# Clearing the record grid, loading the inputs and counting the cells differently in a graph kernel on one Trainium2 core

## The chip, the cores and the metric

The kernel runs on one core of one Trainium2 chip. The metric is the device time of one execution in microseconds (us); of several runs the median is taken. The engines are called as in the profile: PE (matrix multiply), DVE (vector), ACT (scalar), POOL (GpSimd) and SP (the sync engine, which here only issues DMAs). PE's clock has two levels, 1.2 and 2.4 GHz; the profile gives the granted clock of a stretch as a share of the higher one.

## The reference

A graph of 6250 nodes and 200,000 edges, 48 features a node. Cut to what matters:

```
h = relu(layernorm(x))
# first network: a gated message pass, then 4 attention layers over the edges src <- dst
gate = silu(edge_attr @ F1W + F1b) @ F2W + F2b + embedding term of (src, dst)
h = ln(h + segment_sum(gate * h[dst] * cutoff * mult[dst], src) / total)
for i in range(4):
    score = (Q[src] * K[dst]).sum() + 0.1 * (edge_attr * Q[src][:, :40]).sum() + log(mult[dst])
    alpha = segment_softmax(score, src)
    h = ln(h + leaky(concat(h, segment_sum(alpha * h[dst] @ Wm[i], src)) @ Wu[i]))
x = x + h
# second network: 5 steps of a degree-normalised spread over the same edges
out = x + spread(relu(layernorm(x)))
```

## The kernel before, in words

The nodes are cut into 49 blocks of 128 (NB = 49). Each edge belongs to a cell, given by the block of its source and the block of its target, so there are 49 x 49 cells. In device memory stands a grid of records (REC) with room for 128 edges in each cell; a record (RW = 54 floats) holds the edge's 40 attributes and its fields. Everything after the preparation (gate pass, attention layers, spread) reads this grid. The preparation is what the change touches, and it runs through these stages, in the order of the calls at the end of the program:

- load_all (L407 to L465): DVE clears six tiles (L414 to L419), then SP loads 22 pieces of input and weights (L420 to L440). Then come two iotas on POOL, small constants on DVE (L441 to L454), and a few matrix products and reductions on the weights (L456 to L463).
- count_cells (L468 to L545): a tile of zeros is set (L470, 128 x 2646 floats), the edges' sources, targets and weights are loaded (L471 to L473, each 125 partitions x 1600 elements), and DVE takes local index and block number out of them (L474 to L490). Then the histogram: for 200 groups of 8 edge columns, DVE makes two one-hot tiles by comparing a row 0..48 with the block numbers (L503, L504), and PE multiplies them, one product per column (L512, 1600 in all). Two buffers for each tile let DVE run ahead of PE. From the histogram DVE works out base positions (L519 to L539). Then SP writes the zeros tile to the grid, one block row after the other (L541, L542: 49 DMAs of 1323 KB), and one small piece (L543).
- fill_extra (L552): two barriers over all five engines, with a loop between them that runs only where cells overflow.
- place_edges (L561 to L659): 200 iterations. In each, PE and DVE work out the slots of 8 x 125 edges (L594 to L649), ACT copies attributes and fields together into rec_out (L590, L591, from attr_in, which SP loads in 20 pieces, L578), and POOL scatters 8 x 125 records into the grid with 8 indirect DMAs (L655). A slot tile may be at most four iterations ahead of the scatters (L647, L648). A barrier ends it.

What sets the order: nearly all of load_all and count_cells goes through a helper, serial. It numbers the steps by a single semaphore, order, and each step waits until every step before it, on whatever engine, has ended:

```
for who, fn, inc in steps:
    if who == name:
        e.wait_ge(order, count[0])
        fn(e).then_inc(order, inc)
    count[0] += inc
```

A DMA counts 16, and ends when its data have landed. So every DMA of these stages is issued only after the one before it has landed, and the following compute waits for them all. The histogram and place_edges use semaphores of their own.

Of the kernel before, what the change touches and what calls it, by code (L numbers as in the profile page):

```python
# [11 lines left out]
P = 128  # L12
NB = -(-N // P)
# [5 lines left out]
NS = 8  # L19
SC = ET // NS  # L20
# [20 lines left out]
def build(nc, x, src, dst, edge_attr_40, edge_weight, node_type_119, node_vec, Wq, gq, bq, Wk, gk, bk, Wm, Wu, go,  # L41
# [11 lines left out]
    with ctx:  # L53
        def sem(name):
            return ctx.enter_context(nc.semaphore(name))
# [6 lines left out]
        s_hpe, s_hdve = sem("hist_pe"), sem("hist_dve")  # L62
        s_aload = [sem(f"adj_loaded_{k}") for k in range(2)]
# [135 lines left out]
        with scope() as st:  # L199
# [9 lines left out]
            one_bs, one_bd = sb(st, "one_bs", [EP, 2, NS, NB], BF16), sb(st, "one_bd", [EP, 2, NS, NB], BF16)  # L209
# [13 lines left out]
            zeros = sb(st, "zeros", [P, NB * RW])  # L223
# [114 lines left out]
        def program(name, e):  # L338
# [68 lines left out]
            def load_all():  # L407
# [4 lines left out]
                wqk = WQK[:, :, :].rearrange("i l (k o) -> i (l k) o", k=2)  # L412
                steps = [
                    v(lambda e: e.memset(X[:, :, :], 0.0)),  # L414
# [5 lines left out]
                    sy(lambda e: e.dma_start(X[:, 0:NB - 1, :], x_main)),  # L420
                    sy(lambda e: e.dma_start(X[0:TAIL, NB - 1, :], x[(NB - 1) * P:N, :])),
                    sy(lambda e: e.dma_start(MULT[0:TAIL, NB - 1:NB], node_vec[(NB - 1) * P:N].rearrange("(p o) -> p o", o=1))),
                ]
                def mult_main(e):
                    with nc.allow_non_contiguous_dma(reason="one column of node values per block"):
                        return e.dma_start(MULT[:, 0:NB - 1], node_vec[0:(NB - 1) * P].rearrange("(b p) -> p b", p=P))
                steps.append(sy(mult_main))
                for n, w in enumerate((gq, gk, bq, bk, go, bo)):
                    steps.append(sy(lambda e, n=n, w=w: e.dma_start(LP[:, n, :, :].rearrange("p l h -> p (l h)"), flat(w))))
                steps += [  # L430
                    sy(lambda e: e.dma_start(GN[:, 0, :], vec(gn))), sy(lambda e: e.dma_start(GN[:, 1, :], vec(bn))),
                    sy(lambda e: e.dma_start(WQK[:, :, 0:H], Wq.rearrange("l i o -> i l o"))),
                    sy(lambda e: e.dma_start(WQK[:, :, H:2 * H], Wk.rearrange("l i o -> i l o"))),
                    sy(lambda e: e.dma_start(WM[:, :, :], Wm.rearrange("l i o -> i l o"))),
                    sy(lambda e: e.dma_start(WUF[0:H, :, :], Wu[:, 0:H, :].rearrange("l i o -> i l o"))),
                    sy(lambda e: e.dma_start(WU2[:, :, :], Wu[:, H:2 * H, :].rearrange("l i o -> i l o"))),
                    sy(lambda e: e.dma_start(F1[0:RBF, 0:H], F1W)), sy(lambda e: e.dma_start(F2[0:H, :], F2W)),
                    sy(lambda e: e.dma_start(F2[H:KW, :], F2b.rearrange("(o h) -> o h", o=1))),
                    sy(lambda e: e.dma_start(F1B[:, :], col(F1b))),
                    sy(lambda e: e.dma_start(F2B[:, :], F2b.rearrange("(o h) -> o h", o=1))),  # L440
# [13 lines left out]
                    v(lambda e: e.memset(DEG[:, :], 1.0)),  # L454

                    t(many([lambda e, l=l: e.transpose(bank(0)[0:H, l * H:(l + 1) * H], WM[:, l, :], ident[0:H, 0:H]) for l in range(L)])),  # L456
# [7 lines left out]
                ]  # L464
                serial(steps)  # L465


            def count_cells():  # L468
                serial([
                    v(lambda e: e.memset(zeros[:, :], 0.0)),  # L470
                    sy(lambda e: e.dma_start(src_i[:, :], src.rearrange("(p t) -> p t", t=ET))),  # L471
                    sy(lambda e: e.dma_start(dst_i[:, :], dst.rearrange("(p t) -> p t", t=ET))),
                    sy(lambda e: e.dma_start(home[:, :], edge_weight.rearrange("(p t) -> p t", t=ET))),  # L473
                    v(lambda e: e.tensor_copy(fields[:, :, 2], home[:, :])),  # L474
                ])
                for raw, local, block_f, fb in ((src_i, 0, bs_f, 3), (dst_i, 1, bd_f, 4)):
# [16 lines left out]
                HG = NS  # L493
                groups = ET // HG
                iota49 = lambda n: iota_f[0:EP, 0:NB].unsqueeze(1).broadcast_to([EP, n, NB])
                if name == "vector":
                    e.tensor_scalar(iota_f[:, :], iota_f[:, :], 1.0, None, ALU.subtract).then_inc(s_hdve, 1)
                    e.wait_ge(s_hdve, 1)
                    for g in range(groups):
                        if g >= 2:  # L500
                            e.wait_ge(s_hpe, g - 1)
                        c0 = g * HG
                        e.tensor_tensor(one_bs[:, g % 2], iota49(HG), bs_f[:, c0:c0 + HG].unsqueeze(2).broadcast_to([EP, HG, NB]), ALU.is_equal)  # L503
                        e.tensor_tensor(one_bd[:, g % 2], iota49(HG), bd_f[:, c0:c0 + HG].unsqueeze(2).broadcast_to([EP, HG, NB]), ALU.is_equal).then_inc(s_hdve, 1)  # L504
                    e.wait_ge(s_hpe, groups)
                if name == "tensor":
                    for g in range(groups):
                        e.wait_ge(s_hdve, g + 2)
# [52 lines left out]
            def place_edges():  # L561
# [88 lines left out]
                if name == "gpsimd":  # L650
                    for i in range(ITER):
# [1283 lines left out]
            count_cells()  # L1935
            fill_extra()
# [43 lines left out]
```

## Time and profile before

| | us |
|---|---|
| median of 3 runs | 11522.38 (11522.14 to 11533.53) |
| the profiled execution, its own time | 11514.63 |
| its span in the trace | 11512.8 |
| POOL busy | 5678.4 (49%) |
| DVE busy | 7579.4 (66%) |
| PE busy | 9029.0 (78%) |

The span is the time between the first and the last instruction of the profiled execution. Busy times are sums over instructions; an engine that waits is not busy. In the views below a time at the front of a line is the start, counted from the beginning of the span.

### The profile page before, as it was taken

What the parts mean: (1) busy time and instruction counts of PE and PEld (TensorE: products, weight loads), DVE (VectorE), ACT (ScalarE), POOL (GpSimd) and SP (SyncE); (2) the same over time, 40 slices, a digit from 0 to 9 for tenths busy, and PEclk for the clock granted to TensorE, in tenths of its full rate; (3) what the DMA queues carried; (4) which work ended last, traced back from release to release, by engine and by line L of the source; (5) the groups of instructions that cost most, each with busy time, mean ns of one, the idle gap of its engine ahead of it and who ended that gap; (6) DMA issues with size and microseconds to landing.
All of it is one profiled execution on the core that took longest, in us unless ns stands there. A gap on an engine that the chain in (4) does not pass through costs nothing. (4 is left out here: it accounts for less than half of the span.)

```text
span 11512.8 us, 361357 instructions
## 1 busy us (share of the span) xinstructions
PE 9029.0 (78%) x152213; PEld 8186.6 (71%) x152213; DVE 7579.4 (66%) x17807; ACT 4774.7 (41%) x14433; POOL 5678.4 (49%) x7141
## 2 busy tenths in 40 slices
PE   3166666666388888888888599979978997998899
PEld 2165555555377777777777499869978996998899
DVE  6176666666477777777777677667767776776211
ACT  0000000000144444444444377757766775777000
POOL 0077777777222222222222277757756774776000
PEclk9955555555699999999999799979979997998899
DMA  0511111111122222222222267647736773775565
GB/s 16 240 34 31 36 31 32 35 31 31 37 72 76 71 70 74 74 71 70 73 75 71 69 218 220 195 135 218 224 111 217 219 220 106 220 224 166 221 251 221
DMA packets 874542, 1382.84 MB, mean 120 GB/s; under 512 B 120770, under 2 KB 753314, under 8 KB 855769
## 3 DMA queue, kind: packets, MB, share of 16 engines
q1 hardware_dynamic: 796112, 1314.50, 34.1%
q0 software_dynamic: 76800, 45.06, 2.7%
q8 instruction: 1211, 19.84, 0.7%
q14 instruction: 419, 3.43, 0.1%
HBM read 1079.46 MB, written 278.06 MB: 118 GB/s over the span
## 5 line engine op out<-in xcount | busy, mean ns | idle before, releaser
L655 POOL DMA_INDIRECT edge_records<-rec_out,slot_i x1600 | 1910.6, 1194 | 991.8 <-issue 991.5
L1696 ACT ACTIVATE vals<-carry_h,weight 128x49 f32<-128x49 f32 x9604 | 2321.1, 327 | 6.4
L1533 PE MATMUL psum<-TT,hd_t 128*128 128x97 bf16 x28812 | 1538.3, 210 | 148.0 <-DMA hs_t<-one_hots 110.0
L1331 POOL TENSOR_TENSOR vals_g<-vals_g 128x343 f32<-128x343 f32 x343 | 527.3, 1537 | 2216.4 <-ACT vals_g L1314 2216.4
L1533 PEld LDWEIGHTS psum<-TT,hd_t 128*128 128x128 fp8e4 x28812 | 1374.8, 99 | 165.6 <-issue 162.7
L1741 POOL TENSOR_TENSOR vals<-vals 128x343 f32<-128x343 f32 x1372 | 1042.0, 759 | 92.9
L1294 ACT ACTIVATE hots<-psum 128x896 fp8e4<-128x896 f32 x686 | 629.0, 917 | 1040.3 <-PE psum L1138 651.2
L1736 POOL TENSOR_TENSOR vals<-vals 128x343 f32<-128x343 f32 x1372 | 1042.3, 760 | 6.8 <-ACT vals L1696 6.8
L1601 DVE SCALAR_TENSOR_TENSOR xks<-recs,psum 128x343 f32<-128x343 f32 x1372 | 697.0, 508 | 496.7 <-PE psum L1536 486.6
L1536 PE MATMUL psum<-ts,hs_t 128*128 128x49 bf16 x28812 | 985.3, 185 | 44.0 <-issue 43.6
L590 ACT COPY rec_out<-attr_in 125x320 f32<-125x320 f32 x200 | 91.0, 455 | 2185.4 <-DMA edge_records<-rec_out,slot_i 2185.4
L1573 PE MATMUL psum<-vals,hs 128*128 128x147 bf16 x9604 | 885.3, 235 | 45.4 <-POOL vals L1741 23.0
L1261 DVE TENSOR_TENSOR same<-psum,before_e 128x896 fp8e4<-128x896 f32 x343 | 374.5, 1092 | 826.1 <-PE psum L1163 826.1
L1536 PEld LDWEIGHTS psum<-ts,hs_t 128*128 128x128 fp8e4 x28812 | 879.7, 96 | 51.0 <-issue 50.6
L601 PE MATMUL psum<-ident,key_f 125*125 125x125 f32 x1600 | 690.9, 432 | 235.0 <-POOLq L354 235.0
L1682 ACT COPY carry_h<-psum 128x336 f32<-128x336 f32 x1372 | 590.9, 431 | 611.8 <-DVE xks L1601 608.4
L1899 PE MATMUL psum<-g,AJ 128*128 128x144 bf16 x12005 | 762.3, 228 | 73.1 <-POOLq L354 73.1
L1899 PEld LDWEIGHTS psum<-g,AJ 128*128 128x128 fp8e4 x12005 | 761.4, 99 | 74.0 <-POOLq L354 74.0
L607 PE MATMUL psum<-one_bd,one_bs 125*49 125x49 bf16 x1600 | 106.4, 218 | 831.4 <-DVE one_bsT L622 831.4
L610 PE MATMUL psum<-base,one_bsT 49*125 49x98 f32 x3200 | 727.9, 418 | 0.0
L607 PEld LDWEIGHTS psum<-one_bd,one_bs 125*49 125x49 bf16 x1600 | 81.9, 132 | 908.2 <-DVE one_bsT L622 908.2
L1606 DVE TENSOR_TENSOR xks<-xks,psum 128x343 f32<-128x343 f32 x1372 | 698.7, 509 | 34.2
(326 smaller groups left out, 20920.6 us busy)
## 6 DMA issues: line engine op xcount, KB each, us to landing
AJ<-adjacency SPq DMA_DIRECT2D x35, 5488.0 KB, 16.8
recs<-edge_records SPq DMA_DIRECT2D x196, 756.0 KB, 5.8
hs<-one_hots SPq DMA_DIRECT2D x392, 336.0 KB, 3.3
one_hots<-hots SPq DMA_DIRECT2D x343, 336.0 KB, 2.7
recs<-edge_records SPq DMA_DIRECT2D x196, 567.0 KB, 3.8
hd_t<-one_hots SPq DMA_DIRECT2D x196, 448.0 KB, 4.9
hs_t<-one_hots SPq DMA_DIRECT2D x196, 448.0 KB, 4.9
hd_t<-one_hots SPq DMA_DIRECT2D x196, 336.0 KB, 5.1
```

The source lines that it names most:

```text
L601: e.transpose(keyT[0:EP, o:o + EP], key_f[:, col:col + 1].broadcast_to([EP, EP]), ident_e)
L610: last = e.matmul(found_ps[0:EP, o:o + 2 * NB], one_bsT[:, s, :], base[:, s, :, :].rearrange("p a b -> p (a b)"), start=True, stop=True)
L655: e.indirect_dma_start(REC[:, :], bass.IndirectOffsetOnAxis(ap=slot_i[:, i % 4, s:s + 1], axis=0), rec_out[:, (i // 5) % 2, s, i % 5, :], ...
L1533: e.matmul(D(g, c), hd_t[:, p, g, c, :], TD[:, k, g * GC + c, :], start=k == 0, stop=k == 2)
L1536: last = e.matmul(Q(g, c), hs_t[:, p, g, c, :], ts2[:, p, k, :], start=k == 0, stop=k == 2)
L1573: last = e.matmul(bank(7)[:, 0:3 * KW], hs[:, par(back), g, c, :], val_high[:, g * GC + c, :, :], start=g + c == 0, stop=g * GC + c == NB - 1)
L1601: e.scalar_tensor_tensor(xks[:, 0], recs[:, g, :, 0:XW], 0.1, Dall(g)[:, :, 0:KW], ALU.mult, ALU.add).then_inc(dve_link.sem, 1)
L1606: e.tensor_tensor(xks[:, 1], xks[:, 0], Qall(g), ALU.mult).then_inc(multiplied.sem, 1)
L1696: last = e.activation(vals[:, c, 0, :], carry_h[:, par(back), c, :], ACT.Copy, scale=weight[:, par(back), c:c + 1])
L1736: e.tensor_tensor(vals[:, cols(g), 1, :], vals[:, cols(g), 0, :], val_high[:, cols(g), 0, :], ALU.subtract).then_inc(less_high.sem, 1)
L1741: e.tensor_tensor(vals[:, cols(g), 2, :], vals[:, cols(g), 1, :], val_high[:, cols(g), 1, :], ALU.subtract).then_inc(weighted.sem, 1)
L1899: last = e.matmul(spots[:, c * 256:c * 256 + 3 * H], AJ[:, n % 2, bs, c * P:(c + 1) * P], g3[:, now, bs, :, :].rearrange("p k h -> p (k h) ...
```

## The change

The grid is cleared by DMAs that ACT's queue issues from the start of the program. They wait only for the zeros tile and for the three edge arrays (s_ends). The zeros tile becomes 378 floats wide and is read seven times over by each DMA (a broadcast source), where it was 2646 floats wide. The end of the clearing is no longer a step of the serial order; POOL waits for it (s_clear) before the first scatter. SP issues the three loads of edge arrays first, at once, and then, after the DVE clears, the 22 loads of input and weights, without waits in between (s_init). The work on the weights moves into a new function, combine_weights, which runs after count_cells; PE and DVE wait for s_init there. The histogram's groups hold 16 edge columns where they held 8; the one-hot tiles are laid out as block number by column ([EP, NB, HG]) where they were column by block number, all operands of the comparison are bf16 (a copy of the row 0..48, iota_16, and bf16 copies of the block numbers, bs_16 and bd_16), and PE reads each column with a step of 16 elements. place_edges uses the same memory as before under its old names, with its old layout.

```
--- before
+++ after
+HG = 16
+        s_init, s_ends, s_clear = sem("weights_loaded"), sem("edge_ends_loaded"), sem("grid_cleared")
-            one_bs, one_bd = sb(st, "one_bs", [EP, 2, NS, NB], BF16), sb(st, "one_bd", [EP, 2, NS, NB], BF16)
+            hot_bs, hot_bd = sb(st, "hot_bs", [EP, 2, NB, HG], BF16), sb(st, "hot_bd", [EP, 2, NB, HG], BF16)
+            one_bs, one_bd = (h[:, 0, :, :].rearrange("p b j -> p (b j)").rearrange("p (r s b) -> p r s b", r=2, s=NS) for h in (hot_bs, hot_bd))
+            bs_16, bd_16 = sb(st, "bs_16", [EP, ET], BF16), sb(st, "bd_16", [EP, ET], BF16)
+            iota_16 = sb(st, "iota_16", [EP, NB, HG], BF16)
-            zeros = sb(st, "zeros", [P, NB * RW])
+            zeros = sb(st, "zeros", [P, GC * RW])
...
+                serial([
+                    v(lambda e: e.memset(zeros[:, :], 0.0)),
                     v(lambda e: e.memset(MULT[:, :], 1.0)),
...
+                    v(lambda e: e.memset(X[:, :, :], 0.0)),
+                ])
+                if name == "scalar":
+                    e.wait_ge(order, 1)
+                    e.wait_ge(s_ends, 16 * 3)
+                    for b in range(NB):
+                        e.dma_start(rec_rows[b].rearrange("p (g w) -> p g w", g=NG), zeros[:, :].unsqueeze(1).broadcast_to([P, NG, GC * RW])).then_inc(s_clear, 16)
+                    e.dma_start(rec_extra[ZERO], zeros[:, 0:RW]).then_inc(s_clear, 16)
+                if name == "sync":
+                    e.dma_start(src_i[:, :], src.rearrange("(p t) -> p t", t=ET)).then_inc(s_ends, 16)
+                    e.dma_start(dst_i[:, :], dst.rearrange("(p t) -> p t", t=ET)).then_inc(s_ends, 16)
+                    e.dma_start(home[:, :], edge_weight.rearrange("(p t) -> p t", t=ET)).then_inc(s_ends, 16)
+                    e.wait_ge(order, count[0])
+                    e.dma_start(X[:, 0:NB - 1, :], x_main).then_inc(s_init, 16)
...  (the other 21 loads in the same way, as many DMAs as before)
+            LOADS = 22
+
+            def combine_weights():
+                wqk = WQK[:, :, :].rearrange("i l (k o) -> i (l k) o", k=2)
+                if name in ("tensor", "vector"):
+                    e.wait_ge(s_init, 16 * LOADS)
+                serial([ ... the seven steps of L456 to L463 ... ])
...
             def count_cells():
-                serial([
-                    v(lambda e: e.memset(zeros[:, :], 0.0)),
-                    sy(lambda e: e.dma_start(src_i[:, :], src.rearrange("(p t) -> p t", t=ET))),
-                    sy(lambda e: e.dma_start(dst_i[:, :], dst.rearrange("(p t) -> p t", t=ET))),
-                    sy(lambda e: e.dma_start(home[:, :], edge_weight.rearrange("(p t) -> p t", t=ET))),
+                if name == "vector":
+                    e.wait_ge(s_ends, 16 * 3)
...
+                        v(lambda e, block_16=block_16: e.tensor_copy(block_16[:, :], tmp_i[:, :])),
...
-                HG = NS
                 groups = ET // HG
+                    e.tensor_copy(iota_16[:, :, :], iota_f[0:EP, 0:NB].unsqueeze(2).broadcast_to([EP, NB, HG])).then_inc(s_hdve, 1)
+                    e.wait_ge(s_hdve, 2)
-                        e.tensor_tensor(one_bs[:, g % 2], iota49(HG), bs_f[:, c0:c0 + HG].unsqueeze(2).broadcast_to([EP, HG, NB]), ALU.is_equal)
-                        e.tensor_tensor(one_bd[:, g % 2], iota49(HG), bd_f[:, c0:c0 + HG].unsqueeze(2).broadcast_to([EP, HG, NB]), ALU.is_equal).then_inc(s_hdve, 1)
+                        e.tensor_tensor(hot_bs[:, g % 2], iota_16[:, :, :], bs_16[:, c0:c0 + HG].unsqueeze(1).broadcast_to([EP, NB, HG]), ALU.is_equal)
+                        e.tensor_tensor(hot_bd[:, g % 2], iota_16[:, :, :], bd_16[:, c0:c0 + HG].unsqueeze(1).broadcast_to([EP, NB, HG]), ALU.is_equal).then_inc(s_hdve, 1)
-                            last = e.matmul(bank(0)[0:NB, s * NB:(s + 1) * NB], one_bs[:, g % 2, k, :], one_bd[:, g % 2, k, :],
+                            last = e.matmul(bank(0)[0:NB, s * NB:(s + 1) * NB], hot_bs[:, g % 2, :, k], hot_bd[:, g % 2, :, k],
...
-                for b in range(NB):
-                    steps.append(sy(lambda e, b=b: e.dma_start(rec_rows[b], zeros[:, :])))
-                steps.append(sy(lambda e: e.dma_start(rec_extra[ZERO], zeros[:, 0:RW])))
...
                 if name == "gpsimd":
+                    e.wait_ge(s_clear, 16 * (NB + 1))
                     for i in range(ITER):
...
             count_cells()
+            combine_weights()
             fill_extra()
```

## Rows read from the trace of the kernel before

**Rows 1.** The page: POOL's busy tenths in 40 equal slices of the span.

```profile
POOL 0077777777222222222222277757756774776000
```

**Rows 2.** Source views of L655 and L512: count, min/median/max ns, first and last start in us.

```profile
L655 POOL DMA_INDIRECT edge_records<-rec_out,slot_i x1600: 1182/1187/1517, 565.6 to 2962.3; - x178
...
L512 PE MATMUL psum<-one_bd,one_bs x1600: 217/219/243, 115.8 to 306.0; 125*49 125x49 bf16 x178
```

**Rows 3.** Waits view: waiting engine and line, releaser; us in total, times, longest.

```profile
DVE slot_i L649 <- DMA edge_records<-rec_out,slot_i: 246.6, 167, 4.2
```

**Rows 4.** Timeline, all engines, from the start to the first histogram group.

```profile
1.37 2.02 DVE L414 MEMSET X<- 128x2352 f32 x1 [1.37 <-PEq L1973]
...
63.61 0.52 PE L456 MATMUL psum<-ident,WM 48*48 48x48 f32 x4 [63.61 <-DVE DEG L454]
...
67.28 0.55 DVE L463 TENSOR_TENSOR WQK<-WQK,STAT 48x384 f32<-48x384 f32 x1
...
70.73 0.27 SPq L471 DMA_DIRECT2D src_i<-in_src  x1
...
95.42 1.67 DVE L474 COPY fields<-home 125x1600 f32<-125x1600 f32 x1 [24.71 <-DMA home<-in_edge_weight]
...
100.85 0.99 DVE L481 CAST bs_f<-tmp_i 125x1600 f32<-125x1600 int32 x1
...
114.66 0.57 DVE L503 TENSOR_TENSOR one_bs<-iota_f,bs_f 125x392 bf16<-125x392 f32 x1
```

**Rows 5.** Timeline from the last histogram group to the first scatter.

```profile
305.02 0.56 DVE L504 TENSOR_TENSOR one_bd<-iota_f,bd_f 125x392 bf16<-125x392 f32 x1
...
314.46 14.11 SPq L542 DMA_DIRECT2D edge_records<-zeros  x4
...
540.64 0.33 SPq L543 DMA_DIRECT2D edge_records<-zeros  x1
542.32 0.66 DVE L544 MEMSET rec_out<- 125x720 f32 x1 [227.88 <-DMA edge_records<-zeros]
544.77 22.93 SPq L578 DMA_DIRECT2D attr_in<-in_edge_attr  x2
...
565.62 1.41 POOL L655 DMA_INDIRECT edge_records<-rec_out,slot_i  x1 [504.48 <-issue]
```

**Rows 6.** Windows view: length, busy of each engine (instructions), granted clock, DMA share, GB/s.

```profile
150.00:200.00 50.00, 28.71 (x422) 22.28 (x423) 50.00 (x106) 0.00 (x0) 0.00 (x0) 1.00 0.01 1
...
600.00:650.00 50.00, 37.81 (x196) 34.94 (x197) 38.52 (x145) 2.53 (x10) 39.94 (x34) 0.50 0.13 19
...
4.90:12.70 7.80, 0.00 (x0) 0.00 (x0) 0.00 (x0) 0.00 (x0) 0.00 (x0) 1.00 0.68 151
...
4.90:70.70 65.80, 2.03 (x12) 1.67 (x12) 5.99 (x18) 0.00 (x0) 0.37 (x2) 1.00 0.19 31
```

**Rows 7.** DMA view of 319:532 (clearing), 544.8:560.7 (one attr_in load) and 8000:8200.

```profile
q1 hardware_dynamic: 6624, 62.32, 69.7%
...
DMA  0010213223333333333333333333333333333310
...
q1 hardware_dynamic: 1005, 1.60, 27.3%
...
q1 hardware_dynamic: 35721, 43.77, 70.5%
```

**Rows 8.** Timeline of PE: products of one histogram group, and two fp32 products in place_edges.

```profile
200.68 0.55 PE L512 MATMUL psum<-one_bd,one_bs 125*49 125x49 bf16 x8 [0.41 <-DVE one_bd L504]
...
545.37 0.42 PE L601 MATMUL psum<-ident,key_f 125*125 125x125 f32 x1
545.58 0.41 PE L602 MATMUL psum<-ident,bs_f 125*49 125x125 f32 x1
```

**Rows 9.** Groups by line and form: x count, busy us, mean ns, idle before.

```profile
L1386 DVE TENSOR_TENSOR lo_ids<-lo_hot,bad 49x1568 bf16<-49x1568 bf16 x1 | 1.8, 1782 | 0.0
L1387 DVE TENSOR_SCALAR lo_ids<-lo_hot,part_f 49x1568 bf16<-49x1568 bf16 x1 | 1.0, 1022 | 0.0
```

More of the change, by code:

```diff
@@ L411, in load_all @@
                 x_main = x[0:(NB - 1) * P, :].rearrange("(b p) h -> p b h", p=P)
-                wqk = WQK[:, :, :].rearrange("i l (k o) -> i (l k) o", k=2)
-                steps = [
-                    v(lambda e: e.memset(X[:, :, :], 0.0)),
+                serial([
+                    v(lambda e: e.memset(zeros[:, :], 0.0)),
                     v(lambda e: e.memset(MULT[:, :], 1.0)),
@@ L427, in load_all @@
[L427 to L440, printed above, removed]
@@ new lines, in load_all @@
+                if name == "sync":
[4 more added lines that the diff above has]
+                    e.dma_start(X[:, 0:NB - 1, :], x_main).then_inc(s_init, 16)
+                    e.dma_start(X[0:TAIL, NB - 1, :], x[(NB - 1) * P:N, :]).then_inc(s_init, 16)
+                    e.dma_start(MULT[0:TAIL, NB - 1:NB], node_vec[(NB - 1) * P:N].rearrange("(p o) -> p o", o=1)).then_inc(s_init, 16)
+                    with nc.allow_non_contiguous_dma(reason="one column of node values per block"):
+                        e.dma_start(MULT[:, 0:NB - 1], node_vec[0:(NB - 1) * P].rearrange("(b p) -> p b", p=P)).then_inc(s_init, 16)
+                    for n, w in enumerate((gq, gk, bq, bk, go, bo)):
+                        e.dma_start(LP[:, n, :, :].rearrange("p l h -> p (l h)"), flat(w)).then_inc(s_init, 16)
+                    e.dma_start(GN[:, 0, :], vec(gn)).then_inc(s_init, 16)
+                    e.dma_start(GN[:, 1, :], vec(bn)).then_inc(s_init, 16)
+                    e.dma_start(WQK[:, :, 0:H], Wq.rearrange("l i o -> i l o")).then_inc(s_init, 16)
+                    e.dma_start(WQK[:, :, H:2 * H], Wk.rearrange("l i o -> i l o")).then_inc(s_init, 16)
+                    e.dma_start(WM[:, :, :], Wm.rearrange("l i o -> i l o")).then_inc(s_init, 16)
+                    e.dma_start(WUF[0:H, :, :], Wu[:, 0:H, :].rearrange("l i o -> i l o")).then_inc(s_init, 16)
+                    e.dma_start(WU2[:, :, :], Wu[:, H:2 * H, :].rearrange("l i o -> i l o")).then_inc(s_init, 16)
+                    e.dma_start(F1[0:RBF, 0:H], F1W).then_inc(s_init, 16)
+                    e.dma_start(F2[0:H, :], F2W).then_inc(s_init, 16)
+                    e.dma_start(F2[H:KW, :], F2b.rearrange("(o h) -> o h", o=1)).then_inc(s_init, 16)
+                    e.dma_start(F1B[:, :], col(F1b)).then_inc(s_init, 16)
+                    e.dma_start(F2B[:, :], F2b.rearrange("(o h) -> o h", o=1)).then_inc(s_init, 16)
@@ L441, in load_all @@
+                steps = [
                     po(lambda e: e.iota(iota_i[:, :], pattern=[[1, P]], base=1, channel_multiplier=0)),
@@ L454, in load_all @@
                     v(lambda e: e.memset(DEG[:, :], 1.0)),
+                ]
+                serial(steps)
+            LOADS = 22
[3 more added lines that the diff above has]
+                    e.wait_ge(s_init, 16 * LOADS)
+                serial([
                     t(many([lambda e, l=l: e.transpose(bank(0)[0:H, l * H:(l + 1) * H], WM[:, l, :], ident[0:H, 0:H]) for l in range(L)])),
@@ L463, in load_all @@
                     v(lambda e: e.tensor_tensor(wqk, wqk, STAT[0:H, 0, 0:2 * L].unsqueeze(2).broadcast_to([H, 2 * L, H]), ALU.subtract)),
-                ]
-                serial(steps)
+                ])
             def count_cells():
-                serial([
-                    v(lambda e: e.memset(zeros[:, :], 0.0)),
-                    sy(lambda e: e.dma_start(src_i[:, :], src.rearrange("(p t) -> p t", t=ET))),
-                    sy(lambda e: e.dma_start(dst_i[:, :], dst.rearrange("(p t) -> p t", t=ET))),
-                    sy(lambda e: e.dma_start(home[:, :], edge_weight.rearrange("(p t) -> p t", t=ET))),
-                    v(lambda e: e.tensor_copy(fields[:, :, 2], home[:, :])),
-                ])
-                for raw, local, block_f, fb in ((src_i, 0, bs_f, 3), (dst_i, 1, bd_f, 4)):
+                if name == "vector":
+                    e.wait_ge(s_ends, 16 * 3)
+                serial([v(lambda e: e.tensor_copy(fields[:, :, 2], home[:, :]))])
+                for raw, local, block_f, block_16, fb in ((src_i, 0, bs_f, bs_16, 3), (dst_i, 1, bd_f, bd_16, 4)):
                     serial([
@@ L491, in count_cells @@
                 ])
-                HG = NS
                 groups = ET // HG
-                iota49 = lambda n: iota_f[0:EP, 0:NB].unsqueeze(1).broadcast_to([EP, n, NB])
                 if name == "vector":
@@ L507, in count_cells @@
                     for g in range(groups):
-                        e.wait_ge(s_hdve, g + 2)
+                        e.wait_ge(s_hdve, g + 3)
                         for k in range(HG):
```

6 lines of the change are left out of this document (removed).

## The prediction

> **What bounds the kernel now.** I read the slices of the page first. POOL is the engine to see: it does nothing for the first twentieth of the span, and then stands at 7 tenths for eight slices, without a dip [rows 1]. The source view of its line in that stretch gives 1600 scatters, from 565.6 to 2962.3 us [rows 2]. That is 2396.7 / 1599 = 1.499 us from one to the next, of which 1.19 is the instruction and 0.30 a gap that no other engine fills. The view of the waits says the same from the other side: DVE waited in 167 of 200 iterations for scatters of four iterations earlier [rows 3]. So place_edges runs at POOL's own pace. Its length hangs on none of the work that the change touches, and the stages after it begin when it ends. What the change can move is one point, the start of the first scatter at 565.6 us. Call it T.
>
> The timeline, read next, shows what T is made of [rows 4, 5]. SP's chain of small loads and the weight products run to 67.8 (67.28 + 0.55), and 70.7 to 95.4 are three loads one after the other. DVE's preparation runs to 114.7 and the histogram to 305.6. The bases take until 314.5, the grid's clearing until 542.3. A memset and two barriers end at 544.8, and 20.8 us pass to the first scatter: the first attr_in load, then ACT's copies of five iterations. Nothing overlaps in this chain. During the clearing every engine waits for DMAs, 49 of them, issued about every 4.6 us, each behind the landing of the one before [rows 5].
>
> **The change part by part.** I follow two branches that now run side by side and meet at T.
>
> *Edge loads, both branches.* SP issues them at about 1.4 us (the first DVE instruction starts at 1.37 [rows 4]). One after the other they take 24.7 us. How far three in flight overlap no row shows. A DMA of 125 partitions is bound by few of the 16 DMA engines: the load of attr_in keeps the share at a level 3 tenths to its end [rows 7]. If all three loads use the same few engines, only their latencies overlap. A small DMA takes 1.7 us from issue to release 540.64 to 542.32 [rows 5], so three loads take 24.7 - 2 x 1.7 = 21.3. Bounds are 8.2 (a full overlap) and 24.7. I take 21.3, so they land at 22.7. The rule on how many engines a DMA gets, in the Trainium skill (DMA: Bandwidth & Descriptors, "Why a DMA increments its semaphore by 16 and not by 1"), gives a DMA the largest number up to 16 that divides its outer size, and always the lowest-numbered: five for 125 partitions, so the three share the same five. The trace's 3 tenths agree with 5 of 16; if the loads spread evenly instead, T would fall by up to 13 us.
>
> *Compute branch.* The DVE clears (about 4.5 us) and the iotas and constants are over by some 10 us, under the loads; they cost nothing, and 3 us more would cost nothing either. From the landing to the first comparison took 114.66 - 95.42 = 19.2. Added are two casts of 0.99 each (the cast at 100.85) and the widening of the 0..48 row to 784 elements, fp32 in, 0.9 by the spacing of DVE's comparisons (below): 2.9. The histogram starts at 22.7 + 19.2 + 2.9 = 44.8.
>
> The histogram was bound by DVE: it is busy 50.00 of 50 us [rows 6], and 200 groups took 190.9 us, 0.955 each, 0.477 for a comparison of 392 elements. Now there are 100 groups with two comparisons of 784. At one element a cycle each would take 0.477 + 392 x 1.04 ns = 0.885 us (1.04 ns an element from 1782 ns for 1568 at L1386 [rows 9] less about 560 for 392 at L504 [rows 5]), in all 177 us. At two a cycle each takes about 0.478, in all 95.5. No row here has a vector comparison of two bf16 inputs. The tensor_scalar of 1568 bf16 elements took 1022 ns, and the tensor_tensor beside it, one of whose inputs is fp32, 1782 [rows 9]: two a cycle is there for bf16 alone, and one fp32 operand loses it. In the change no operand is fp32, so I take 95.5. The Trainium skill (VectorE: DVE Perf Modes, "The perf-mode tier table") has the same for this operation: twice the rate where all three tensors are 16-bit in SBUF with step one, and no more.
>
> PE's 8 products of a group lie within 0.55 us [rows 8], and one alone lasts 0.219 [rows 2], so they start (0.55 - 0.219) / 7 = 47 ns apart. 16 take 0.76 us, under the 0.955 of a DVE group; without any overlap of two halves it would be 1.10, 110 us in all, and hidden as well. PE now reads with a step of 32 bytes. No row has such an operand; the rival below prices it.
>
> So the histogram ends at 44.8 + 95.5 = 140.3, and then 8.9 (305.58 to 314.46) for the bases, 0.7 for the memset, 4.2 for the moved weight work (63.61 to 67.83 [rows 4]) and 1.8 of barriers (542.98 to 544.77) bring place_edges to 155.9. With 20.8 behind it, this branch alone would give T = 176.7. The 22 loads of weights are done long before: alone they fill 0.19 of 65.8 us, 12.5 us of DMA time [rows 6].
>
> *Clearing branch.* It begins at 22.7. Its bytes are 49 x 128 x 10584 = 66.4 MB, 4.15 MB for each of 16 DMA engines. The packets shrink from up to 10584 B to 1512 B. The rate of a busy engine, bytes over time times share times 16, is 62.32 MB / (213 x 0.697 x 16) = 26.2 GB/s in the old clearing; 1.60 / (15.9 x 0.273 x 16) = 23.0 for attr_in with packets of 1600 B; and 43.77 / (200 x 0.705 x 16) = 19.4 in the attention stage, with packets of 1225 B on the mean [rows 7]. That is 158, 180 or 214 us for the clearing. I take 23.0, the row nearest in size, 180. The gain over 227.9 us comes from dropping the wait between DMAs: the old share was 0.70.
>
> Other traffic shares the engines: the loads behind the edge arrays, up to 12.5, of which I count 8; and on the few engines that serve it, attr_in's first two pieces. SP issues the first at 155.9, the second after ACT's ten copies, both inside the clearing. One keeps its engines busy for about 14 us (15.9 less latency), so 28 more. That gives 22.7 + 180 + 8 + 28 + 1.7 = 240. If instead ACT must wait for room in its queue while it issues 50 DMAs, it reaches the barriers only near the end of the clearing (212). Then attr_in comes after, and T is about 212 - 5 + 20.8 = 228. I take T = 235 between the two.
>
> *Behind T.* POOL's pace stays. The barrier at the end, the gate pass and all that follows have the same instructions. PE starts place_edges without 230 us of rest, but the pace doesn't depend on its clock: at 600 to 650 us the granted clock was 0.50 (the 1.2 GHz level) and POOL was busy for 39.94 of 50 us as ever [rows 6].
>
> *Sum.* T moves from 565.6 to 235, so 331 us are saved, with the span from 11512.8 to 11182. The profiled execution took 11514.6; the median of the runs is 11522.4, 7.8 above. Against the median: 11522.4 - 331 = 11191.
>
> **The rivals.** *DVE stays at one element a cycle.* For: no row shows the pairing of two bf16 inputs. The histogram ends at 44.8 + 177 = 222, T = 222 + 15.6 + 20.8 = 258, and the time is 11522 - 307 = 11215. The clearing (over by 215 without attr_in beside it) is hidden then.
>
> *PE's strided reads become the bound.* For: both operands step over 32 bytes; nothing in the trace does. Fp32 products of 125 columns follow each other after 0.21 us [rows 8], 1.67 ns a column, four times the cycle at 2.4 GHz. At that rate for 49 columns a read takes 82 ns; the product beside its weight load gives a histogram of 131 us and costs nothing; both in a row, 164 ns, give 262. Then T = 44.8 + 262 + 36.4 = 343, and the time is 11300. It decides from about (235 - 36.4 - 44.8) / 1600 = 96 ns a product. The Trainium skill speaks against this layout (Advanced Engine Details and Errata, "Memory Cachelines"): SBUF is read in lines of 16 bytes, and an access pattern that touches a new line each time pays a penalty. By that rule the histogram lies between 95.5 and 262; no run here shows the size of the penalty.
>
> *The clearing is slow.* At 14 GB/s for each engine, the rate of the x load with its pieces of 192 B (151 / (0.68 x 16) [rows 6]), it takes 296 us, T is about 330 and the time 11287. Issued from another queue, with 49 completions as before, it could also keep the old 228: T about 270, 11227.
>
> *The other side: slower than before.* The scatters lose POOL's pace. If an iteration of DVE and PE, now 8 x 1.499 = 12.0 with a DVE wait of about 246.6 / 200 = 1.2 us [rows 3], grew by more than 1.2 + 331 / 200 = 2.9 us, the gain would be gone. The one-hot tiles of place_edges lie in new addresses with the old layout; I see no cause. At +4 us it would be 11522 - 331 + 560 = 11751.
>
> **How the numbers follow.** Forecast 0.70; DVE at one a cycle 0.12; PE bound 0.09; slow clearing 0.06; the other side 0.03. The forecast's own range: T from 205 (26.2 GB/s, and nothing beside it) to 262 (19.4), time 11162 to 11219. It holds the first rival. With the half of the next two that lies near, and for runs that differ by 11 us, the range is 11150 to 11245. A measurement of this kernel tells about 0.2% (23 us) from no change; All cases but the last are faster: 0.96, with 0.01 kept for no change and 0.03 for slower.
>
> **What would show it.** Right: the first scatter near 235 with 1.50 us between scatters; s_clear as the last to come; comparisons of 784 elements spaced by 0.48 us; GB/s in the clearing near 370 with a DMA share of 9 tenths. Wrong: comparisons of 0.89; PE's products spaced by over 0.06 us with DVE waiting for PE; a last scatter more than 2400 us after the first.

## The result, and the profile after

| | before | changed kernel |
|---|---|---|
| median (lowest to highest), us | 11522.26 (11521.66 to 11533.53), 4 runs | 11252.56 (11224.86 to 11256.88), 4 runs |
| profiled execution, its span, us | 11514.63, 11512.8 | 11249.7, 11247.9 |
| first scatter (T), us | 565.6 | 276.9 |
| last scatter, us | 2962.3 | 2685.0 |

The ratio is 0.9759 (95% interval 0.9742 to 0.9776), 2.4% faster. Predicted was 11191, with a range up to 11245: the median lies 62 us above the one and 8 us above the other. The gain is 270 us where 331 were forecast. One execution in this study, the fourth of the kernel with two pieces below, took 18860.59 us for a reason that isn't known, and no ratio counts it.

The source view of the scatters in the changed kernel (count, min/median/max ns, first and last start in us) is the first thing to read, beside [rows 2]:

```profile
L675 POOL DMA_INDIRECT edge_records<-rec_out,slot_i x1600: 1182/1187/1598, 276.9 to 2685.0; - x178
```

The profiled executions differ by 11512.8 - 11247.9 = 264.9 us. T moved by 288.7 us. Place_edges takes 2408.1 us where it took 2396.7, 11.4 back. From the last scatter to the end of the span pass 8562.9 us where 8550.5 passed, another 12.4 back. Instructions there are the same, and over all profiled executions of this study the stretch lay between 8550 and 8587, so I read nothing into it. So the forecast missed T by 42 us, and what lies behind T by 24, of which place_edges is 11.

The timeline of the changed kernel shows T's two branches; ACTq and SPq are the queues' own issuing, whose length is how long the engine was held. It answers to [rows 4, 5].

```profile
0.81 0.38 SPq L433 DMA_DIRECT2D src_i<-in_src  x1
...
23.80 1.68 DVE L496 COPY fields<-home 125x1600 f32<-125x1600 f32 x1 [15.52 <-DMA home<-in_edge_weight]
23.86 27.34 ACTq L430 DMA_DIRECT2D edge_records<-zeros  x8
...
27.72 3.61 SPq L441 DMA_DIRECT2D MULT<-in_node_vec  x1
...
31.38 32.80 SPq L443 DMA_DIRECT2D LP<-in_gq  x1
...
46.09 0.57 DVE L525 TENSOR_TENSOR hot_bs<-iota,bs 125x784 bf16<-125x784 bf16 x1
46.57 0.56 DVE L526 TENSOR_TENSOR hot_bd<-iota,bd 125x784 bf16<-125x784 bf16 x1
...
198.46 0.56 DVE L541 COPY hist<-psum 49x392 f32<-49x392 f32 x1 [1.98 <-PE psum L534]
...
211.39 0.55 DVE L489 TENSOR_TENSOR WQK<-WQK,STAT 48x384 f32<-48x384 f32 x1
244.14 5.39 ACTq L431 DMA_DIRECT2D edge_records<-zeros  x1
...
251.38 1.00 SPq L597 DMA_DIRECT2D attr_in<-in_edge_attr  x1
...
271.91 1.28 ACT L609 ACT_TABLE_LOAD   x1 [271.91 <-DMA attr_in<-in_edge_attr]
...
276.87 1.41 POOL L675 DMA_INDIRECT edge_records<-rec_out,slot_i  x1 [271.00 <-issue]
```

The source view of ACT's issuing (ns min/median/max, first and last start in us; then us from issue to landing):

```profile
L430 ACTq DMA_DIRECT2D edge_records<-zeros x49: 655/4427/8463, 23.9 to 240.3; - x49
...
DMA to landing us min/median/max: 8.9/18.8/26.0
```

The compute branch is over at 211.9 (211.39 + 0.55), and then DVE stands still until 251.4: ACT issues the small last DMA of the clearing until 244.14 + 5.39 = 249.5, and only then reaches the barriers. Behind the barriers the attr_in load, issued at 251.4, lands at 271.9, and 5.0 us of ACT's copies lead to the first scatter. So it is the case "ACT held by its queue" of the prediction's clearing branch, later than priced.

The histogram did not run as forecast either. The windows of the changed kernel (busy PE, PEld, DVE, ACT, POOL with instructions, granted clock, DMA share, GB/s), beside [rows 6], and its waits:

```profile
50.00:100.00 50.00, 50.00 (x533) 50.00 (x532) 34.45 (x67) 0.00 (x0) 0.00 (x0) 1.00 1.11 282
100.00:150.00 50.00, 50.00 (x532) 50.00 (x532) 34.45 (x66) 0.00 (x0) 0.00 (x0) 1.00 1.07 298
```

```profile
DVE hot_bs L525 <- PE psum L534: 46.1, 98, 0.9
```

PE, not DVE, is busy for 50.00 of 50 us. 533 products in 50 us are 94 ns each at a granted clock of 1.00, the 2.4 GHz level; the forecast had 47. DVE's two comparisons start 0.48 us apart, as forecast, and it waited for PE 98 times.

The DMA view of the changed kernel from 60 to 200 us (packets, MB, share of 16 engines), beside [rows 7]:

```profile
q10 hardware_dynamic: 27138, 40.32, 102.6%
q1 hardware_dynamic: 4194, 0.85, 4.4%
```

q10 is the clearing. 40.32 MB / (140 us x 1.026 x 16) = 17.5 GB/s for each busy engine, where [rows 7] gave 26.2 for the same bytes in packets of up to 10584 B. The engines are full now, and the packets are slower: 140 x 1.026 x 16 / 27138 = 85 ns for 1512 B.

### The profile page after: what moved, and what is told of

Its sections match the earlier page's. It is cut to its first block and busy times, and to the rows that moved or that the text cites. A ratio compares the mean times of both kernels' runs of the same rounds, so it can differ in the third digit from the quotient of the medians.

```text
span 11247.9 us, 361165 instructions
## 1 busy us (share of the span) xinstructions
PE 9080.7 (81%) x152213; PEld 8263.3 (73%) x152213; DVE 7494.7 (67%) x17610; ACT 4775.3 (42%) x14433; POOL 5689.6 (51%) x7141
## 5 line engine op out<-in xcount | busy, mean ns | idle before, releaser
L626 PE MATMUL psum<-hot_bd,hot_bs 125*49 125x49 bf16 x1600 | 106.5, 218 | 848.3 <-DVE one_bsT L641 848.3
L626 PEld LDWEIGHTS psum<-hot_bd,hot_bs 125*49 125x49 bf16 x1600 | 81.9, 132 | 924.8 <-DVE one_bsT L641 924.8
```

## The experiments

Each ran beside the kernel before on the same chip; ratios are to that, with the 95% interval. Medians are over four runs unless said otherwise. The kernel that an edit is made to is the changed kernel, or "whole rows" (the first experiment) where said.

**Whole rows.** Is the clearing slow through its packets' size? The same DMAs, with the source as wide as a row of the grid:

```
-zeros = sb(st, "zeros", [P, GC * RW])
+zeros = sb(st, "zeros", [P, NB * RW])
-e.dma_start(rec_rows[b].rearrange("p (g w) -> p g w", g=NG), zeros[:, :].unsqueeze(1).broadcast_to([P, NG, GC * RW]))
+e.dma_start(rec_rows[b], zeros[:, :])
```

> The changed kernel, with a zeros tile of 2646 floats and no repeated source, so that each row of the grid is written in pieces of 10584 bytes as before. Theory (small packets): in the changed kernel the clearing moves 306 GB/s at a DMA share of 1.07, so the engines are full and each 1512-byte packet is dear; the old clearing had 26.2 GB/s for a busy engine. With the old packets and no waits the clearing takes about 160 us plus the loads, the ACT queue has issued its last DMA before 200 us, and the histogram's end (198) sets the barrier at about 214 us. The first scatter then starts at 235 to 240 us where it started at 276.9, and the time is about 38 us lower than the changed kernel's. Rival (device memory takes no more than about 300 GB/s of writes): the clearing keeps its rate, the first scatter stays at 277 us and the time at the changed kernel's.

Measured: 11202.49 us against 11530.86, ratio 0.9716 (0.97 to 0.9732); T at 236.2. Its DMA view from 60 to 150 us, and one window with the columns as above:

```profile
q10 hardware_dynamic: 3973, 37.33, 98.9%
q1 hardware_dynamic: 3972, 0.02, 2.5%
```

```profile
100.00:150.00 50.00, 50.00 (x533) 50.00 (x532) 34.61 (x67) 0.00 (x0) 0.00 (x0) 1.00 1.02 417
```

37.33 MB / (90 x 0.989 x 16) = 26.2 GB/s for each engine, the rate of before. ACT is through at 166.2 us, and the clearing has landed before 200. Now the compute branch sets T, and PE's histogram, which ends at 198.7, is what it waits for. This version is about 50 us faster than the changed kernel (0.9759 - 0.9716 = 0.0043 of 11530), and no later version is faster beyond the noise: this is the one to keep.

**Two pieces.** Is it the size of a packet, or that the source is read over and over? Here packets are half a row and the source is still read twice (`zeros` of NB * RW // 2 floats, g=2).

> The changed kernel, with a zeros tile of 1323 floats read twice over: the source is still repeated, the pieces are 5292 bytes. Theory (size of a packet): 10584 bytes in 404 ns and 1512 bytes in 86 ns give 33 ns a packet and 28.5 GB/s for the rest, so 5292 bytes take about 219 ns, 24 GB/s for an engine, and the clearing about 172 us plus the loads; the first scatter starts at 235 to 245 us. Rival (the repeated source itself is slow, as each repetition reads the same bytes): the rate stays near 17.5 GB/s for an engine and the first scatter near 277 us.

Measured: ratio 0.9717 (0.9698 to 0.9737) over three runs, 11198.13, 11211.65 and 11223.83 us, T 236.2. From 60 to 150 us its clearing shows

```profile
q10 hardware_dynamic: 6840, 34.07, 96.3%
```

34.07 / (90 x 0.963 x 16) = 24.6 GB/s with 5292 B: the size it is, not the repeated source.

**Attributes early.** Can the attr_in load be taken out from behind the barrier? SP issues the first one behind the edge arrays, and the loop in place_edges starts with the second.

```
+e.dma_start(attr_in[:, :, :, :].rearrange("p s i r -> p s (i r)"), edge_attr_40.rearrange(...)[:, :, 0:JB * RBF]).then_inc(s_edges, 16)
-for b in range(ITER // JB):
+for b in range(1, ITER // JB):
```

> The changed kernel, with the first load of edge attributes issued by SP right behind the three edge arrays, and no longer after the barriers. Theory (the barriers are held by ACT, which cannot finish issuing the clearing before about 250 us; behind them a load of 16 us, the ACT table load and five copies are exposed): the barriers stay near 250 us or come up to 14 us later, the first scatter follows them after 11 to 12 us, when the first slots are there, and starts at 262 to 272 us; 5 to 15 us are saved. Rival (the wait for the cleared grid ends last): the first scatter stays at 277 us or later.

Measured: 11260.26 us against 11530.86, ratio 0.9763 (0.9747 to 0.978), T 281.3: no gain, and the expected T was missed. The copies did start 1.3 us behind the barrier, and the first scatter followed 14.3 us behind it (at 267.05, where DVE's first instruction of place_edges starts) instead of 25.5. What is late next is DVE's and PE's first iteration, whose slots were ready at 280.1 (the timeline of this run):

```profile
267.05 0.57 DVE L638 TENSOR_TENSOR hot_bs<-iota_f,bs_f 125x392 bf16<-125x392 f32 x1 [57.04 <-POOLq L359]
...
279.98 0.17 DVE L670 TENSOR_TENSOR slot_i<-slot_a,slot_b 125x8 int32<-125x8 f32 x1
```

So 11 us were won. But ACT is held by its queue until 265.2, 16 us longer than in the profiled execution of the changed kernel. That same unchanged issuing ended at 257.8 in a second execution of the changed kernel (last experiment) and at 259.3 with the old histogram (next one), so 8 to 10 of the 16 us can be what the clearing varies by; the rest may be the load that now runs beside it. Which, is not settled.

**Old histogram.** Everything of the change but the histogram: groups of 8, fp32 operands, columns side by side, as in [rows 6] and [rows 8].

> The changed kernel, with the histogram as in the kernel before (groups of 8 columns, fp32 comparisons, tiles that PE reads without a step). Theory (the clearing hides the histogram): it takes 191 us again and ends at about 234 us, 36 us later than in the changed kernel, place_edges still begins at about 250 us, and the time stays within 6 us of the changed kernel's. Rival (the histogram sets the start): the time grows by 36 us or more.

Measured: 11246.36 us, ratio 0.9754 (0.9738 to 0.977), T 285.6. The histogram ran to 235.0, 190 us, and nothing was lost: it was still over before ACT reached the barriers (259.3). T is 8.7 us later than in the profiled execution of the changed kernel, by the clearing, and place_edges takes 10.5 us less (2397.6). In this change the new histogram is worth nothing.

**Histogram alone.** The kernel before with the new histogram and nothing else.

> The kernel before with the new histogram alone (groups of 16 columns, bf16 comparisons, PE reading with a step of 32 bytes); loads and clearing stay as they were. Theory (PE is the bound of the new histogram, 94 ns a product): it takes 151 us instead of 191, less 3 us for the added casts, so the first scatter comes 37 us earlier than in the kernel before. A second effect is in question: with the new histogram place_edges took 2408 to 2410 us in three kernels, with the old one 2397 and 2398. If the histogram brings that about, place_edges takes about 2408 here and the whole saves 26 us; if the ACT clearing or the loads do, it takes 2397 and the whole saves 37 us.

Measured: 11519.82 us against 11551.16 (10 and 13 runs), ratio 0.9975 (0.9965 to 0.9984), 29 us faster, T 535.4 for 565.6. The histogram took 151 us (120.5 to 271.7) here too: PE's 94 ns are its own, not the clearing's beside it. On a serial chain 30 of the 40 us by which the histogram is shorter reach T; 37 were expected. Place_edges took 2402.1 us, between the 2397 and the 2408 of the two cases, so this run doesn't say which part of the change makes it longer.

**Eight and four columns.** Does PE's step cause the 94 ns? Both on whole rows, with HG = 8 (a step of 16 bytes) and HG = 4 (8 bytes).

> The kernel with whole rows cleared in pieces of 10584 bytes, where the histogram sets the start of place_edges, and with groups of 8 columns: PE reads with a step of 16 bytes instead of 32. Theory (every element in a new 16-byte line is what costs): the products stay 94 ns apart, the histogram at 151 us and the time unchanged. Rival (the longer step costs): the products come closer together, DVE with 0.27 us a comparison becomes the bound, the histogram takes 110 us, and the first scatter starts up to 40 us earlier, as far as the clearing allows (about 12 us).

> As the kernel with whole rows cleared in pieces of 10584 bytes, with groups of 4 columns: PE reads with a step of 8 bytes, two elements of an operand in each 16 bytes. Theory (the 16-byte line): the products of a group are 47 to 50 ns apart, as without a step, and DVE is the bound with 0.17 us a comparison, 138 us in all. Rival (any step costs): the products stay 94 ns apart and the histogram takes 150 us or more.

Measured: 11230.55 us, ratio 0.9723 (0.9707 to 0.9739), T 252.6, and 11249.87 us, ratio 0.9744 (0.9728 to 0.976), T 266.8. PE's timeline inside a group of eight columns, and with four columns:

```profile
99.91 0.82 PE L534 MATMUL psum<-hot_bd,hot_bs 125*49 125x49 bf16 x7
...
100.50 0.73 PE L534 MATMUL psum<-hot_bd,hot_bs 125*49 125x49 bf16 x8 [0.18 <-DVE hot_bd L526]
101.42 0.73 PE L534 MATMUL psum<-hot_bd,hot_bs 125*49 125x49 bf16 x8 [0.18 <-DVE hot_bd L526]
```

With eight columns one product lasts 0.27 us, so seven in 0.82 us start (0.82 - 0.27) / 6 = 92 ns apart. The medians over all groups are 92 ns at 16 bytes and 49 ns at 8 bytes (44 in the trace before). In both kernels T is later than with whole rows all the same: the histogram lasts from 46.9 to 216.0 and from 46.2 to 230.0, 169 and 184 us, where 151 and 138 were expected. DVE's comparisons, spaced by 0.28 and 0.17 us, come to 112 and 140 us in all; the rest is the two engines waiting for each other between groups, which smaller groups do more often (PE 200 times with four columns, once with 16). So only the step of 8 bytes frees PE, and small groups take back more than it gives.

**One operand.** Does one stepped operand do it? On whole rows, the first ten groups get 48 further products each, into banks that nobody reads: only the stationary operand stepped (L540), only the moving one (L542), neither (L544).

> The kernel with whole rows cleared in pieces of 10584 bytes; in the first ten groups of the histogram PE makes 48 more products, whose results nobody reads: 16 with the stationary operand alone in steps of 32 bytes, 16 with the moving operand alone, 16 with neither. Theory (each operand has its own read and the slower one sets the pace): about 94 ns between products with either operand stepped, 44 with none. Rival (only the weight load suffers): 94 ns with the stationary operand stepped, 44 with the moving one stepped. A third way (both share one read): 70 ns with either.

One run: 11239.76 us. PE's timeline of the first group:

```profile
47.09 1.74 PE L534 MATMUL psum<-hot_bd,hot_bs 125*49 125x49 bf16 x16 [47.09 <-DVE hot_bd L526]
48.65 1.65 PE L540 MATMUL psum<-hot_bd,hot_bs 125*49 125x49 bf16 x16
50.12 1.61 PE L542 MATMUL psum<-hot_bd,hot_bs 125*49 125x49 bf16 x16
51.55 0.92 PE L544 MATMUL psum<-hot_bd,hot_bs 125*49 125x49 bf16 x16
52.30 1.70 PE L534 MATMUL psum<-hot_bd,hot_bs 125*49 125x49 bf16 x16
```

From start to start: 16 products with both operands stepped take 1.56 us, with the stationary one 1.47, with the moving one 1.43, with neither 0.75. Either operand alone is enough.

**Quads.** Groups of 16 for DVE and a step of 8 bytes for PE: tiles of four quads, on whole rows.

```
-hot_bs = sb(st, "hot_bs", [EP, 2, NB, HG], BF16)
+hot_bs = sb(st, "hot_bs", [EP, 2, 4, NB, HG // 4], BF16)
-e.matmul(..., hot_bs[:, g % 2, :, k], hot_bd[:, g % 2, :, k], ...)
+e.matmul(..., hot_bs[:, g % 2, k // 4, :, k % 4], hot_bd[:, g % 2, k // 4, :, k % 4], ...)
```

> The kernel with whole rows cleared in pieces of 10584 bytes, with groups of 16 columns whose one-hot tiles are laid out in four parts of 4 columns ([EP, 4, NB, 4]), so that DVE still makes 784 elements with an instruction and PE reads with a step of 8 bytes. Theory (PE pays when each element lies in another 16 bytes: 44 ns between products without a step, 49 at 8 bytes, 92 at 16 and 94 at 32): the products are 49 ns apart, DVE with 0.955 us a group is the bound again, the histogram takes 96 to 100 us instead of 151, and place_edges begins when ACT has issued its last clearing, near 168 us; the first scatter starts between 196 and 205 us, 30 to 40 us earlier than with the 32-byte step. Rival (runs of 4 elements break the doubled rate of DVE): 0.89 us a comparison, 177 us in all, and a first scatter at about 262 us.

Measured: 11207.17 us against 11535.78, ratio 0.9712 (0.9696 to 0.9728), T 228.9. The histogram took 105.5 us, from 47.3 to 152.8, where 96 to 100 were expected, with the products 49 ns apart and DVE nearly always busy (47.2 of 50 us). T was missed by 24 to 33 us. A window, four lines of the timeline and one of the waits of this run say why:

```profile
50.00:100.00 50.00, 45.72 (x760) 40.40 (x758) 47.20 (x96) 0.00 (x0) 0.00 (x0) 1.00 1.02 416
```

```profile
42.66 137.08 SPq L443 DMA_DIRECT2D LP<-in_gq  x1
...
161.24 0.66 DVE L563 MEMSET rec_out<- 125x720 f32 x1 [0.22 <-DVE base L561]
...
200.63 0.51 PE L482 MATMUL psum<-ident,WM 48*48 48x48 f32 x4 [44.26 <-DMA F2B<-in_F2b]
...
206.71 24.27 SPq L597 DMA_DIRECT2D attr_in<-in_edge_attr  x2
```

```profile
PE psum L482 <- DMA F2B<-in_F2b: 44.3, 1, 44.3
```

SP was held for 137 us at one issue, behind the load of MULT (L441), which brings 48 x 128 = 6144 elements of 4 B in as many packets. The DMA view of this run from 60 to 150 us shows how the two queues share:

```profile
DMA packets 7919, 37.38 MB, mean 415 GB/s; under 512 B 4395, under 2 KB 4395, under 8 KB 4395
...
q10 hardware_dynamic: 3953, 37.17, 98.7%
q1 hardware_dynamic: 3954, 0.02, 2.5%
```

As many packets of the one queue as of the other: they take turns, one for one (also in every single microsecond of the 90 the counts differ by 2 at most). Of q10's packets 4395 - 3954 = 441 are small too, and 3512 have 10584 B. On the mean a turn of q10 takes 90 x 0.987 x 16 / 3953 = 0.36 us. The 6144 packets of MULT on 16 engines are 384 for each, and every one waits for such a turn: 138 us in all, and SP is held for 137.08. So the weights landed at 200.6. The compute branch had been ready for them at 161.9 (161.24 + 0.66), and combine_weights began 39 us late. Of the 46 us by which the histogram is shorter than with whole rows, T shows 7. In the changed kernel a turn costs 85 ns, 384 x 0.085 = 33 us, and SP is held for 32.80. Loading MULT ahead of the clearing should set this free; that wasn't tried.

**Quads, attributes early.** The early attr_in load added to quads.

> As the kernel with quads, and the first load of edge attributes issued by SP behind the three edge arrays. Theory (the last landing of the clearing is the bound now, and the load in front of it delays it on the few engines that serve it): the clearing lands 10 to 14 us later, at about 208 us, and the first scatter starts there; nothing gained, up to 10 us lost against the kernel with quads. Rival (the exposed load counts): the first scatter comes up to 10 us earlier than without.

Measured: 11214.16 us, ratio 0.972 (0.9704 to 0.9736), T 230.4: no gain. SP now issued the last of the weights' loads at 209.2 us, where quads alone issued it at 198.4, so the barriers moved back by what the load won. The theory on record had the clearing's last landing as the bound; it was the weights, as in quads alone.

**Comparison of two tensors.** Place_edges is 11 us longer than before. In the trace before, 50 of its 1599 distances between scatters are over 1.53 us; after, 95 are, each longer by some 0.24 us: 45 x 0.24 = 11 us. 94 of the 95 lie over DVE's tensor_scalar from psum (one_bsT, L641). Whole rows with that instruction as a tensor_tensor:

```
-e.tensor_scalar(one_bsT[...], bsT[...], part_f[0:NB, 0:1], None, ALU.is_equal)
+e.tensor_tensor(one_bsT[...], bsT[...], part_f[0:NB, 0:1].broadcast_to([NB, 4 * EP]), ALU.is_equal)
```

> The kernel with whole rows cleared in pieces of 10584 bytes, and in place_edges the comparison that makes one_bsT written as an operation of two tensors (the second repeated along the row) instead of a tensor_scalar with a per-partition scalar. Theory (this tensor_scalar holds up POOL: of the 95 scatters of the changed kernel that start more than 1.53 us before the next one, 94 overlap it): the long scatters go to under 10, place_edges takes about 1599 x 1.492 = 2386 us where it took 2408, and the time falls by 22 us. Rival (only the phase of the two engines, any DVE work there would do it): about as many long scatters as before, and place_edges stays at 2395 to 2410 us.

Measured: 11220.8 us against 11551.16, ratio 0.9719 (0.9703 to 0.9736), and the theory fell: 101 long distances, 100 of them over that instruction, and place_edges at 2405.9 us.

**The changed kernel again**, beside quads.

> The changed kernel once more, on the same chip as the kernels with quads, to compare them with it there: first scatter near 277 us, ratio to the kernel before about 0.976.

Measured: 11262.38 us against 11535.78, ratio 0.9763 (0.9744 to 0.9782), T 285.0, ACT's issuing to 257.8. The first result stands, and T of the changed kernel varies by some 8 us with the clearing.

## Why the prediction was right or wrong

**Right: one point, T, carries the gain.** T gave 288.7 us, of which 24 were lost again behind it: 264.9. POOL's pace went from 1.499 to 1.506 us. The forecast of three serial loads for the edge arrays (landed at 23.8, forecast 22.7) and of the compute branch up to the first comparison (46.1 for 44.8) held. So did 0.48 us for a comparison of 784 elements; the rival "DVE stays at one element a cycle" is out.

**The term that was mis-sized, and that cost the time: the clearing's rate.** The forecast took 23.0 GB/s an engine from the attr_in load, the row nearest in size, and 180 us. It was 17.5. In the case where ACT is held, the clearing was to be over at 212 and T at 228. The last full DMA was issued at 240.3 and the last small one landed 16.5 us after 244.14, at 260.7; ACT reached the barriers at 249.5 (207 forecast), 42 us late. The load behind them took 20.5 us for 15.9, beside the clearing's last packets, and the copies 5.0: T = 251.4 + 20.5 + 5.0 = 276.9. So s_clear, which the forecast named as the last to come, was 16 us ahead of the first scatter. The clearing lasts 260.7 - 23.9 = 237 us, and took 227.9 before: what the dropped waits gave, the smaller packets took back. That is the case "keeps the old 228" of the rival on slow clearing, priced at T = 270, by another mechanism than the one named there. The bound from the attention stage, 19.4 GB/s, was closer, and 17.5 lay below even this. Whole rows settle it: with one edit to the source tile the rate is 26.2 GB/s and ACT is through at 166.2. That T is then 236.2, next to the 235 of the forecast, is luck: the histogram sets it there, and the forecast had the clearing set it.

By T alone the median would have been near 11522 - 289 = 11233, inside the range. The 24 us behind T, which the forecast put at nothing, carried it over the edge; 12 of them are within what executions differ by.

The Trainium skill (DMA: Bandwidth & Descriptors, "Specifications") has 512 B as the size from which a transfer runs at line rate. The runs here differ: 1512 B gave 17.5 GB/s an engine, 5292 B 24.6, and 10584 B 26.2, so the measurement decides.

**A second step that failed, at no cost here: PE's pace.** The forecast carried 47 ns a product over from [rows 8], where a column's elements lie side by side. With a step of 32 bytes it was 94, and the histogram took 151 us for 95.5. The second rival had the mechanism, and named 96 ns as the pace from which it decides. 94 is just under, and it stayed hidden: the compute branch was over at 211.9 against ACT's 249.5. That this error didn't show in the time is luck. Under whole rows the cover is gone, and PE sets T. The steps of 8, 16 and 32 bytes gave 49, 92 and 94 ns, and either operand alone was enough: the cause is shown.

This agrees with the Trainium skill (Advanced Engine Details and Errata, "Memory Cachelines"), by which SBUF is read in lines of 16 bytes and a line should serve at least two accesses: at 8 bytes two bf16 elements that are read share a line, at 16 each has its own.

**Not foreseen: place_edges 11 us longer.** The forecast saw no cause for it, and named a last scatter over 2400 us after the first as a sign of being wrong: 2408.1 were measured. The pieces are located, but the cause isn't found. About as many scatters lie over DVE's comparison from psum as before (220, and 235 in the trace before); more of them are long. Kernels with the old histogram, with eight or four columns, or with before's order have 50 to 68 long distances and 2397 to 2402 us; those with 16 columns and ACT's clearing have 92 to 104 and 2406 to 2410. It isn't that instruction's form. The two traces do show that it goes with how DVE stands to POOL. Where an iteration's first such comparison starts between 0.1 and 1.4 us after a scatter's start, a long scatter lies over it or the second one nearly always: 47 of 47 iterations before, 85 of 88 after. In the other iterations it is 2 of 151 and 9 of 109. So the changed kernel has 88 such iterations where there were 47. What shifts the engines against each other, and why a scatter is long then, is open.

**What the gain consists of.** Not of faster work: the clearing takes as long as before, and the histogram's new form is worth nothing here and 29 us alone. It comes from the clearing, the loads and the compute lying beside one another where they lay in a row.

## What to carry to other kernels

When work leaves a serial chain, it is worth the chain only down to the end of the next branch: price every branch to its own end, and count an engine that issues many large DMAs as held for about as long as they move. Look at the packet size before the waits: the smaller packets cost here as much as the 49 waits did. Lay a bf16 operand of PE out so that its step stays at 8 bytes or less, and keep loads made of many small pieces off the time in which another queue moves large packets.

## What the runs showed of the hardware

- A packet of the clearing took 85 ns at 1512 B and 0.40 us at 10584 B, on the mean of full DMA engines; the core wrote 416 GB/s with the large ones, and 295 with the small.
- Two queues on the same DMA engines took turns packet by packet, whatever their size (3953, of which 3512 of 10584 B, against 3954 of 4 B in 90 us). A load of 24 KB in 4-byte pieces held SP for 137 us beside packets of 10584 B, and for 33 us beside 1512 B.
- ACT was held for 4.4 us on the median by the issue of each of the 49 DMAs, about the time that 1323 KB take at the 295 GB/s of this stretch (4.6 us), with the data landing 18.8 us after the issue. That it waited for room in the queue is the reading of this; no view shows the queue's room.
- PE's products of 49 columns in bf16 start 44 to 47 ns apart on the median with elements side by side, 49 with steps of 8 bytes, and 90 to 94 with steps of 16 or 32 bytes, one operand or both, at the 2.4 GHz level all of them.
- DVE's comparison of 784 bf16 elements is spaced by 0.48 us, as one of 392 elements with fp32 inputs was, also with inner runs of only four elements (in the quads).
